# Attention values in bursts of eight heads, a new memory plan for w2, and new places for the pieces

## What is computed

```python
x = x + attn(layernorm(x))                          # 16 heads of 16, rope on q and k, bias, softmax
x = x + xattn(ctx, ctx, layernorm(x), mask) @ W_fc.T  # 16 heads of 16, keys and values are ctx itself
x = x + ffn(layernorm(x))                           # 8 experts, the best 2 of each row:
#   h = gelu(x @ w1[e] + b1[e]);  y = h @ w2[e] + b2[e];  sum of top_p[e] * y over the 2 experts
```

## Time and profile before

| | us |
|---|---|
| median of 3 runs | 746.16 |
| lowest, highest | 743.03, 747.18 |
| the profiled execution, its own time | 748.79 |
| its span, first to last instruction | 746.8 |
| PE busy in the span | 647.2 |
| DVE busy | 352.2 |
| ACT busy | 403.3 |
| POOL busy | 286.5 |

### The profile page before, as it was taken

One profiled execution on the slowest core, in us unless ns is written; L12 is line 12 of the kernel. 1 busy time (PEld: TensorE's weight loads), 2 busy tenths in 40 slices (PEclk: granted clock), 3 DMA queues, 4 the chain that ended last, 5 costly groups with the idle time before them and its releaser, 6 DMA issues.

```text
span 746.8 us, 15196 instructions
## 1 busy us (share of the span) xinstructions
PE 647.2 (87%) x4859; PEld 517.3 (69%) x4859; DVE 352.2 (47%) x812; ACT 403.3 (54%) x872; POOL 286.5 (38%) x543
## 2 busy tenths in 40 slices
PE   3475798798998999989858877889999999999996
PEld 3344576465765666666535566779999999999995
DVE  1385767587786887868753411521121121212111
ACT  3443557567575687778436642534545545454551
POOL 3222315335045355454264541543342433334332
PEclk9697999899999999999888988999999999999999
DMA  5646466557676576875965892132222212122221
GB/s 129 131 106 150 97 136 142 141 114 155 138 162 151 141 160 160 184 181 133 254 139 91 209 216 57 16 29 40 43 32 41 39 34 43 29 44 34 39 29 22
DMA packets 57597, 78.26 MB, mean 105 GB/s; under 512 B 12877, under 2 KB 51152, under 8 KB 54448
## 3 DMA queue, kind: packets, MB, share of 16 engines
q1 hardware_dynamic: 48552, 66.61, 39.4%
q0 software_dynamic: 8512, 10.26, 9.1%
q10 hardware_dynamic: 456, 0.42, 0.2%
HBM read 54.52 MB, written 22.35 MB: 103 GB/s over the span
## 4 chain that ended last, share of the span: by engine, by line
PE 55%; DMA 14%; POOL 10%; issue 7%; DVE 5%; SPq 5%; ACT 4%; ACTq 0%; POOLq 0%; DVEq 0%
PE attention_psum L676 16%; PE attention_psum L669 16%; PE attention_psum L661 5%; DMA xs<-in_x 5%; PE attention_psum L621 4%; PE attention_psum L634 4%; PE attention_psum L706 3%; DMA out<-over 2%; DMA weights<-in_L_ffn_w 2%; SPq L512 2%; DMA weights<-parts 2%; POOL lists L1321 2%; PE attention_psum L572 2%; POOL weights L1400 2%; PE attention_psum L578 2%
## 5 line engine op out<-in xcount | busy, mean ns | idle before, releaser
L1127 DVE TENSOR_REDUCE neg_max<-attention_psum 128x2 f32<-128x512 f32 x256 | 167.4, 684 | 68.1 <-PE attention_psum L621 67.5
L829 ACT ACTIVATE weights<-attention_psum 128x512 f32<-128x512 f32 x256 | 149.6, 596 | 73.0 <-PE attention_psum L634 71.9
L676 PE MATMUL attention_psum<-weights,xs 128*128 x624 | 143.7, 384 | 8.3 <-issue 6.7
L669 PE MATMUL attention_psum<-over,v 128*128 128x128 f32 x1248 | 150.5, 280 | 0.0
L669 PEld LDWEIGHTS attention_psum<-over,v 128*128 128x128 f32 x1248 | 146.8, 196 | 0.7 <-issue 0.4
L916 ACT ACTIVATE xs<-attention_psum,b_sb 128x128 f32<-128x128 f32 x312 | 89.3, 369 | 91.0 <-PE attention_psum L669 91.0
L676 PEld LDWEIGHTS attention_psum<-weights,xs 128*128 128x128 f32 x624 | 117.4, 193 | 23.5 <-issue 8.7
L1391 POOL DMA_INDIRECT out<-over x39 | 63.2, 1620 | 169.6 <-DVE over L1185 155.5
L621 PE MATMUL attention_psum<-weights 99*128 99x256 bf16 x512 | 103.4, 286 | 27.9 <-DVE neg_max L1127 13.6
L1179 DVE TENSOR_TENSOR over<-attention_psum,b_sb 128x256 f32<-128x256 f32 x39 | 16.6, 425 | 206.6 <-PE attention_psum L676 205.2
L634 PE MATMUL attention_psum<-weights 102*128 102x256 bf16 x512 | 101.5, 281 | 1.1 <-ACT weights L829 1.0
(11 more groups left out here) (163 smaller groups left out, 708.2 us busy)
## 6 DMA issues: line engine op xcount, KB each, us to landing
parts<-weights SPq DMA_DIRECT2D x96, 128.0 KB
weights<-parts SPq DMA_DIRECT2D x32, 384.0 KB
weights<-parts SPq DMA_DIRECT2D x32, 256.0 KB
weights<-in_L_ffn_w SPq DMA_DIRECT2D x8, 1024.0 KB, 11.7
weights<-parts SPq DMA_DIRECT2D x32, 128.0 KB
w_sb<-in_L_ffn_w SPq DMA_DIRECT2D x8, 512.0 KB, 3.6
weights<-in_L_ffn_w SPq DMA_DIRECT2D x8, 512.0 KB, 9.3
xs<-in_x SPq DMA_DIRECT2D x8, 256.0 KB, 8.4
```

The source lines that it names most:

```text
L669: last = pe.matmul(m.hT_bank[j % 2][:, c * P:(c + 1) * P], m.w1t[j % 2][:, k, c * P:(c + 1) * P], m.xT[j % 2][:, k, :], start=(k == 0), st ...
L676: last = pe.matmul(m.bank_of(("down_a", TILE, j))[:, 0:D], m.hidT[j % 2][:, c, :], m.w2_sb[:, bass.ds(expert, 1), c, :].rearrange("p a n - ...
L829: act.activation(m.p[:, u % P_RING, :], m.b_bank[u % B_RING], ACT.Exp, scale=SCALE[ORDER[u // H][0]]).then_inc(m.b_free[u % B_RING], 1)
L1127: v.tensor_reduce(m.neg_max[:, :, h:h + 1], m.a_bank[u % A_RING].rearrange("p (t k) -> p t k", t=T), AXX, ALU.max, negate=True).then_inc(m ...
```

## The change

It has six parts, of which the tables are one:

1. `TOGETHER` 4 to 8 and `P_RING` 8 to 12. A burst holds the values of eight heads, in slots 4 and 12 of a unit, the first four heads' matmuls before the others'.
2. Memory: `xs` moves into `weights`, partly under w2; w2 starts lower; the stacks come behind `xs`, then two groups of four exponential buffers; the third group, `p_last`, is a tensor of its own and later holds b2. Expert 0 of w2 waits for the stored rows of X3, experts 1 to 6 each for one of the last three units' exponential scores, expert 7 for the values of all but eight heads. `hidT` lies behind w2.
3. b2 is loaded in one DMA of 1 MB, in slot 277, when all values are done; the eight DMAs of slot 192 go.
4. The stacks of the first two units are loaded in halves of eight heads, twelve DMAs instead of six; the first head waits for the first half only, head 8 for the rest.
5. At the start the q projection waits for wq alone, k for wk, v for wv (before: for seven DMAs together), and DVE for the biases and the rope table.
6. All tables of slots have new numbers; the first two units have tables of their own. The w2 loads stand in slots 243, 249, 249, 264, 263, 276, 275, 275 (before 246, 249, 262, 265, 278, 279, 280, 281).

```diff
-TOGETHER = 4
-P_RING = 8
+TOGETHER = 8
+P_RING = 12
...
-W1_AT, W1_EVERY, W2_AT = 231, 3, (246, 249, 262, 265, 278, 279, 280, 281)
+W1_AT, W1_EVERY, W2_AT = 231, 3, (243, 249, 249, 264, 263, 276, 275, 275)
...
+        self.weights = sb("weights", [P, E * F + half + w2 + 4 * BANK])
...
+        self.xs = self.weights[:, E * F:E * F + 2 * half].rearrange("p (n d) -> p n d", d=D)
+        self.w2_sb = self.weights[:, E * F + half:E * F + half + w2].rearrange("p (e c d) -> p e c d", e=E, c=FC)
...
+        self.p_last = sba("p_last", [P, 4, BANK])
+        under = [under([P, 4, BANK]), under([P, 4, BANK]), self.p_last]
+        self.p = [under[g][:, k, :] for g in (1, 0, 2) for k in range(4)]
...
-                for e in range(E):
-                    sp.dma_start(m.b2_sb[:, e, :], b2[e:e + 1, :].broadcast_to([P, D])).then_inc(m.s_b2, 16)
+            elif name == "b2":
+                sp.wait_ge(m.s_values, len(ORDER) * H)
+                sp.dma_start(m.b2_sb, b2.rearrange("(a e) d -> a e d", a=1).broadcast_to([P, E, D])
+                             ).then_inc(m.s_b2, 16)
...
+                heads = slice(piece[4] * HALF, (piece[4] + 1) * HALF) if i < 2 else slice(0, H)
...
+                                 ).then_inc(m.s_first_heads[i] if heads.stop == HALF else m.s_stack[r], 16)
...
-                if n < E - 2:
-                    u = (len(ORDER) - STACKS + n // 2 + 1) * H - 1
+                if n == 0:
+                    sp.wait_ge(*m.stored(m.s_out, BATCH_ENDS[0] - 1))
+                elif n < E - 1:
+                    u = (len(ORDER) - STACKS + (n - 1) // 2 + 1) * H - 1
                     sp.wait_ge(m.b_full[u % B_RING], u // B_RING + 1)
                 else:
-                    sp.wait_ge(m.s_values, len(ORDER) * H)
+                    sp.wait_ge(m.s_values, len(ORDER) * H - TOGETHER)
...
-        if h == 0:
+        if h == 0 and i < 2:
+            pe.wait_ge(m.s_first_heads[i], 16 * (len(Q_LOADS) + len(K_LOADS)))
+        if h == (0 if i >= 2 else HALF):
             pe.wait_ge(m.s_stack[r], 16 * plan.loaded[ORDER[i]])
...
-        for t in range(T):
-            for u in units:
+
+        for first, t in ((f, t) for f in units[::4] for t in range(T)):
+            for u in range(first, first + 4):
...
-                        pe.wait_ge(m.s_qkv, 16 * 7)
+                        pe.wait_ge(m.s_wq, 16)
...
-                        act.wait_ge(*m.stored(m.s_out, BATCH_ENDS[0] - 1))
+                        act.wait_ge(m.s_values, len(ORDER) * H)
```

More of the change, by code:

```diff
@@ new lines @@
+BOTH_AT = ((-20, "stack", 0), (-19, "rest", 0), (-18, "mid", 0), (-17, "stack", 1), (-17, "rest", 1), (-17, "write", 0),
+        (-16, "mid", 1), (-14, "write", 1), (-12, "read", 0), (-12, "read", 1), (10, "max_parts", 0), (11,
+        "max", 0), (11, "max_rows", 0), (15, "max_parts", 1), (18, "max", 1), (20, "max_rows", 1))
+FIRST_AT = ((-33, "ln_a", 0), (-30, "ln_d", 0), (-29, "turn"), (-26, "qk_a", 0), (-25, "qk", 0), (-25, "rope", 0), (-25,
+        "qk_a", 1), (-24, "qk", 1), (-22, "rope", 1), (-21, "roped", 0), (-21, "roped", 1), (-21, "v", 0), (-20,
+        "v", 1), (-20, "stack", 0), (-19, "rest", 0), (-18, "mid", 0), (-18, "stack", 1), (-17, "rest", 1),
+        (-17, "write", 0), (-16, "mid", 1), (-14, "write", 1), (-13, "read", 0, 0), (-12, "read", 1, 0), (-12,
+        "read", 0, 1), (-9, "read", 1, 1))
@@ L199, in put @@
         def put(at, name, *more):
-            slots[z + at + (6 if unit == ORDER[1] and at < 0 else 0)].pieces.append((name, a, n, *more))
+            slots[z + at].pieces.append((name, a, n, *more))
+        if z < 2 * H:
+            for at, *piece in (FIRST_AT, SECOND_AT)[POS[unit]]:
+                slots[at].pieces.append((piece[0], a, n, *piece[1:]))
         for table, lag in (((SELF_AT, CROSS_AT)[a], 0), (BOTH_AT, 0), ((AFTER_SELF, AFTER_CROSS)[a], LAG), (AFTER, LAG)):
@@ L220, in schedule @@
                             ("down_a", 0), ("down_b", 0), ("moved_y", 0), ("add", 0)):
-            for k in range(j + ahead, j + ahead + 1):
-                if k < N_TILES and (name not in ("list", "gather") or k > EARLY + 1):
-                    slots[STEADY_AT + j - STEADY].pieces.append((name, TILE, k))
+            if j + ahead < N_TILES and (name not in ("list", "gather") or j + ahead > EARLY + 1):
+                slots[STEADY_AT + j - STEADY].pieces.append((name, TILE, j + ahead))
             if name == "list" and j == EARLY - 4:
@@ L306, in for_attention @@
         self.ctx_keep = under([P, T, D])
+        under = Arena(self.weights[:, E * F + NT * D:])
         self.stack = [None] * STACKS
@@ L387, in signals @@
             [sem(f"{what}_{w}") for w in "qk"] for what in ("cast_hi", "cast_mid", "third", "parts_written"))
+        self.s_first_heads = [sem(f"first_heads{i}") for i in range(2)]
         self.s_stack = [sem(f"stack_loaded{r}") for r in range(STACKS)]
```

109 lines of the change are left out of this document (57 added, 52 removed).

## The result

The changed kernel is **slower: 764.43 us** (median of 4 runs, 762.08 to 767.5) against 746.02 (743.03 to 747.18) for the kernel before in the same series; ratio 1.026, 95% interval 1.021 to 1.031. The prediction said 721, 711 to 733, and gave slower a chance of 0.03. The profiled execution took 766.6 us, span 764.6, which is 17.8 more span than before.

What follows compares the result with a forecast made beforehand. PE was taken to bound the steady tiles, its waits and lowered clock the gains elsewhere; passage 18, routing 3.5, start 5, attention -1 sum to 25.5 us, forecasting 721 us, range 711 to 733.

Steps and rivals of the forecast that it cites:

- Steady attention: Attention units with bursts of eight: gains and losses nearly cancel, net 1 us lost, bounds +6 and -12.
- The term for the turns: Before four self units, slot 0's burst no longer stands under PE's wait of about 2.2: 2 us lost.
- The term for VectorE: In attention, VectorE stands still 0.6 a burst and PE waits later: 19 us at most, 3 taken.
- The slower rival: VectorE and ScalarE fall behind in every attention burst, 38 us lost there: 12.5 slower in all, 759 us; chance 0.03.
- The gain of 0.09 a burst: In attention, each of 32 bursts saved spares 0.09 us: 2.9 at most, bounds 0 and 3.
- The start: First projection waits for less and halved stacks land earlier, S1's wait of 5.75 shrinking: 5 us gained, bounds 1 and 8.
- Routing: First batch's routing: PE's wait for X7's max_parts shortens from 5.90, choose comes earlier: 3.5 us gained, bounds 0 and 6.
- the alternative that the prediction gave beside its own: First batch's routing: X7's first max_rows would wait behind two w2 experts in ring order; gain near 0, sum 3.5 smaller.
- The passage: Passage to the experts: earlier w2 and X6's rows, reordered work removing waits and low clock: 18.6 us, 18 taken.
- The gather of tile 8: Last wait of the passage: the gather lands 1.7 us after PE is ready, so 1.2 of 2.89 goes.
- The steady tiles: Expert tiles after the passage: PE alone bounds them, nothing to gain, again about 243 us long.
- What would show it wrong: Stated signs of error: PE's span from slot 32 to the last attention unit grows over 5, or w2 lands after 445.

Runs made afterwards that it cites:

- The joined pair: Changed kernel with bursts of four, xbias at 15, list at 261, b2 at 283: fours of slots 0/4 joined, 757.44 us; those of 8/12 joined, 748.41 us.
- the run with scores inside the burst: Changed kernel with the next slot's scores for the maxima issued between the two fours of each burst of eight: 763.5 us, ratio 1.021.
- the same repeats: Changed kernel with the scores_for_exp matmuls issued twice in four slots per unit: ahead of the bursts 765.15 us, right behind them 778.19 us.

## Why the prediction was wrong, step by step

- **Steady attention: the step that failed.** Net 1 us lost was forecast, bounds 6 gained to 12 lost; it was some 24. The burst of eight makes 15.8 of them with `xbias` in slot 14, as in the changed kernel. Of the 8.5 that are left with bursts of four, `xbias` makes 6.3, and the prediction had no term for its new slot. (With `xbias` in slot 15 in both, the burst makes 22.3.) Both loss terms, 2 for the turns and 3 for VectorE, were too small, for one reason. The term for the turns saw that "the burst of slot 0, which stood under that wait, is now in slot 4", but counted four self units at 1.0, halved to 2. The joined pair shows a loss far beyond four turns, 15.7 us at slot 0 and 6.1 at slot 8 up to X3's `rturn`, and the timeline shows slot 0's burst under a wait for VectorE. The term for VectorE, 32 x 0.6 with 3 taken "since DVE has 56 us to spare in 203", used the slack of a mean: VectorE had it during the bursts and not in the slots between them, and the run with scores inside the burst shows that the standing still was not the price. The slower rival had the right sign and VectorE in it, and its 759 stands nearest to the measured 764; but that is luck. It has 38 us lost in the bursts themselves, in a form that the run with scores inside the burst speaks against, and gains of 27.5 elsewhere that did not come.
- **The clock had no term in steady attention.** Lower clock was priced in the passage alone; here it went from 0.97 to 0.89 between 87 and 355 us, and 6.5 us of the burst's 22.3 are matmuls that ran longer.
- **The gain of 0.09 a burst** can't be seen: a matmul of values took 460 ns in the changed kernel and 410 before, in the mean.
- **The start: right in mechanism, forecast too large.** 5 was forecast; head 0 of S1 came 3.5 earlier, and the stack is waited for no more. The next wait was not about 3 but 0.46 and 1.73, both for VectorE.
- **Routing.** The wait for X7's `max_parts` fell from 5.90 to 1.79, where "near 2" was said, and that for `chosen` (the output of `choose`) from 2.82 to 2.08. The term as a whole was 5.4 lost and not 3.5 gained (X3 to X5, 53.9 before and 59.3 after), since the first `max_rows` landed late. With the two experts behind these rows the same stretch took 48.3, so that the gain was there, 5.6 us, and the late rows took more than all of it. This was the alternative that the prediction gave beside its own, from the Trainium skill, DMA: Bandwidth & Descriptors, Queues, rings and completion order. The trace agrees with the rule: 12 KB took 13 us behind two experts, and with these behind it the wait was gone. That no exponential score waited for `max_rows` before was rightly held to decide nothing: there the last expert ahead of these rows was issued 7.9 us before them (385.69 and 393.58), here two were issued 7.5 us before, with half an expert of w1 right behind. What the text feared of the `list` ahead of the second rows did not show.
- **The passage: half of it came.** 18 forecast, 8.4 measured (from X6's `rturn` +26.1 to +17.7). X6's rows went from 2.82 to 0.76; the 1.45 and 1.56 are gone. w2 did not: 5.62 waited and 6.66 for the first `down`, as before 6.7 and 6.22. The step took the issue as 9 us earlier and "in by 440 to 443", some 16 to 18 us for three experts; against the first `down` the issue is 21.7 ahead (449.91 to 471.62), 18.5 before. The third expert came with it: w2 was in only 20.6 after the first issue (470.52), and TensorE was there after 16.1. b2 was priced as covered, at up to 3 if not; no run shows what it cost.
- **The gather of tile 8**: a wait of 1.7 forecast, 4.78 measured, 2.89 before. The chain was seen, its shift was not: the second batch's `listed` starts 21.5 us later than before (476.10 and 497.57), the first `down` 20.1.
- **The steady tiles**, 243.5 us, are as forecast. The parts add up to the result: 3.5 - 24.3 - 5.4 + 8.4 = -17.8, where 5 - 1 + 3.5 + 18 = 25.5 was forecast.
- **What would show it wrong** named attention first, more than 5 us, and w2 after 445. Both came, the second partly because everything stood later.

## What to carry to other kernels

Before a burst is moved, ask of each place where it stands now which engine the others wait for there: what lies under another chain is free, and the same work a few slots later can cost all of itself (0 and 13 us here for the same repeats). An engine's spare time in a mean over many slots says nothing for the slots in which it is the bound; read them one by one, in a timeline, with rings of two banks above all. And a wait that an edit takes away in a passage bound by DMA comes back at the next consumer, so count the bytes up to the last one.

## What the hardware showed that was not expected

Two idle times of TensorE of 1.78 us, with bursts of four and `xbias` in slot 14, were followed by a granted clock of 0.68 and 0.53 over the next 10 us. With `xbias` one slot later they were 0.84 us, and the clock behind them was 1.00. In the kernel before with `xbias` in slot 14, the same two waits of 1.77 and 1.78 us were followed by 1.00 and 0.83. So a wait of this length may cost itself or, by an estimate from the 0.68 and 0.53, 3 to 5 us more. Three DMAs of 4 KB landed 13 us after the issue of the last, behind 2.5 MB of weights. And work that TensorE did ahead of its bursts, 14 us of it, cost nothing, in good part because the granted clock rose from 0.89 to 0.93.
